# A fused graph and expert layer on one core: the head's clearing, statistics and copies in another order

## The chip, the cores and the metric

The kernel runs on one core of a Trainium2 chip. Its five engines are TensorE (PE), VectorE (DVE), ScalarE (ACT), GpSimd (POOL) and SyncE (SP); each works through its own instruction stream in order, and they wait for each other through semaphores. Transfers run on 16 DMA engines. SP and ACT put theirs on hardware queues (q1 and q10 in the profile), POOL puts its indirect ones (gathers and scatters by a list of row numbers) on q0. The metric is the device time of one execution in microseconds (us), lower is better. Times of the trace are counted from the start of the profiled span.

## What is computed

6250 nodes with 256 features each, 100,000 edges (src, dst) sorted by dst. First a graph layer, then a mixture of 8 experts of which each row uses the best 2:

```python
def gnn(h, edge_index, W, b):
    msg_sum = segment_sum(h[src], dst, num_segments=n)
    deg = segment_sum(ones, dst, num_segments=n)
    agg = msg_sum / maximum(deg, 1.0)[:, None]
    return concatenate([h, agg], axis=1) @ W.T + b

x = x + gnn(layernorm(x), stack([src, dst]), W, b)
x = x + ffn(layernorm(x)[None], gamma, beta, Wr, br, W1, b1, W2, b2)[0]
# ffn: logits = xn @ Wr + br; top 2; softmax of the two;
#      y = sum over chosen experts of w * (gelu(xn @ W1[e] + b1[e]) @ W2[e] + b2[e])
```

## The kernel before, in words

The nodes lie in 49 tiles of 128 rows (`NT` = 49; the last has 106). The program has a **head** (the five functions `sync_head`, `scalar_head`, `gpsimd_head`, `tensor_head`, `vector_head`) and a **stream** (`..._stream`), one loop over steps `t` that every engine runs in step with the others. There is no scheduler: the order on every engine is the order in which the code is written, and all waits are written out by hand.

In the stream's first 830 steps the sums over edges are made. Each step takes 128 edges: POOL gathers the 128 source rows of the normalised features out of the DRAM tensor `h_rows` (L631), PE multiplies them with a one-hot matrix of the edges' targets (L737), DVE adds the 128x257 result to the accumulator `acc` of the target tile (L1080; column 257 counts edges). The first 96 steps are of a special kind: two steps share one gather (48 gathers, into `shared`). From then on each step has its own gather, at most 17 ahead of the adds. DVE makes the one-hot matrices for 8 or 9 steps at a time (`one_hot`, L972). When a tile's sums are complete, the graph layer's product (L750), the second normalisation, the choice of experts, and later the experts themselves (L805, L830) follow for it between the steps. The rest of the stream hangs on the steps by fixed distances in `t`, so that nothing of it starts by the clock.

The head has three strands, which meet before the first gather of the stream:

- **The index strand.** POOL writes four index tables (`iotas`, L606 to L609) and clears all of `acc` (L610). DVE builds constants out of the tables (L866 to L875), then waits for `s_fst`, the first target of each block of 128 edges, which ACT's queue has loaded with L510 and L512 (672 and 109 elements of 4 bytes each). From L877 on, DVE and PE by turns work out where each tile's edges begin, until DVE writes `e_idx` (L933). In between DVE does the statistics of x tiles. POOL then gathers the edge tables, 8 gathers out of `comb` into `tab_i` (L616). They are converted to floats (targets by DVE, L954; sources by ACT, L537), transposed by PE (L706, L711) and written by DVE as `rel` (L960) and `srcs` (L964). The signal `srcs_up` says that `srcs` is there.
- **The normalisation strand.** SP loads x in 7 groups of 7 tiles (L439, L441). For each group `tile_stats` on DVE takes the statistics (7 + 7 instructions, L842 and L847), ACT takes the root (L526), `tile_scales` on DVE the reciprocal and the product (L854, L855; it stands after the second L842 of the next group), ACT writes 7 normalised tiles into one of two staging buffers `hst` (L532) and SP stores them to `h_rows` (L444). ACT waits at group b for the store of group b-2, whose buffer it fills again (L529).
- **The copies.** After the seven stores SP copies x to the DRAM tensor `x_rows` in seven parts (L447), which the graph layer reads later. POOL's stream waits for all seven stores, for `srcs_up` and for the second half of the transposed targets (L619 to L622). SP's stream waits for all copies before its first loads for the steps (L458).

## Time and profile before

| | us |
|---|---|
| runs, median of 3 | 1489.25 |
| runs, lowest and highest | 1487.42 and 1489.82 |
| the profiled execution, its own time | 1490.06 |
| its span (first to last instruction) | 1488.7 |
| PE busy | 1152.6 |
| POOL busy | 1082.9 |
| DVE busy | 770.8 |
| ACT busy | 496.9 |
| TensorE clock granted, mean | 0.907 |

The profiled execution took 1490.06 us, 1.36 us more than its span and 0.81 us more than the median of the runs. Busy time says how much an engine had to do; the head and the stream have different limits, so what the change is worth is read in the head, from which event released which. The rows of a timeline give start, duration, engine, line and operation, and in brackets how long the engine sat idle before and what released it. The name behind "q" (SPq, ACTq) is an engine's issue of a DMA; "us to landing" is from the issue to the arrival.

### The profile page before, as it was taken

Reading aid. Unit: us, or ns where it says so; the run is one execution under the profiler, and the core shown is the slowest. Engines: PE = TensorE matmul, PEld = TensorE weight load, DVE = VectorE, ACT = ScalarE, POOL = GpSimd, SP = SyncE. Lnnn points to the kernel's source line nnn. Section 1 sums busy time; section 2 is a strip of 40 time slices with the busy share of each in tenths; the row PEclk is TensorE's granted clock in tenths of the full one; section 3 lists DMA queues with packets and bytes.
Section 4 is the critical chain, followed back from the end, with each engine's and each line's share of the span. In section 5 each row is a group of like instructions: output and inputs, shape, how many; then the busy total and the mean of one; then the engine's idle time right before and its main releaser. Section 6 shows DMA issues by size and latency. Waiting matters only on the chain.

```text
span 1488.7 us, 22997 instructions
## 1 busy us (share of the span) xinstructions
PE 1152.6 (77%) x5570; PEld 876.0 (59%) x5570; DVE 770.8 (52%) x2634; ACT 496.9 (33%) x1095; POOL 1082.9 (73%) x1032
## 2 busy tenths in 40 slices
PE   3167888868876987688888768888897878877895
PEld 2033444536643776466667647666676766656794
DVE  8646654555564456435645544644646455554321
ACT  2400001303210453044336214414353434335573
POOL 3377477777777777777777777777777777773777
PEclk9999999789976999789999879979999998988998
DMA  8773475444434454444445454544555454453443
GB/s 257 223 258 106 141 221 182 127 125 136 119 115 130 134 136 114 121 132 119 134 122 136 113 128 127 133 116 124 135 122 128 121 130 123 121 125 92 71 68 40
DMA packets 125080, 197.46 MB, mean 133 GB/s; under 512 B 23954, under 2 KB 94023, under 8 KB 124711
## 3 DMA queue, kind: packets, MB, share of 16 engines
q0 software_dynamic: 63088, 130.30, 35.7%
q1 hardware_dynamic: 58325, 64.36, 13.8%
q10 hardware_dynamic: 3538, 1.34, 0.3%
q8 instruction: 50, 0.82, 0.2%
q14 instruction: 79, 0.65, 0.1%
HBM read 153.82 MB, written 49.27 MB: 136 GB/s over the span
## 4 chain that ended last, share of the span: by engine, by line
PE 44%; POOL 18%; issue 14%; DVE 11%; DMA 7%; ACT 3%; DVEq 1%; ACTq 0%; POOLq 0%; SPq 0%
PE psum L737 15%; PE psum L805 10%; PE psum L830 8%; POOL work L631 8%; DMA work<-h_rows,srcs 4%; PE psum L750 4%; DVE acc L1080 3%; POOL queue L640 3%; POOL region L631 2%; POOL out_dram L651 2%; POOL out_dram L659 2%; DMA out_dram<-expert_buf,tok_idx 1%; PE psum L751 1%; PE psum L784 1%; PE psum L817 1%
## 5 line engine op out<-in xcount | busy, mean ns | idle before, releaser
L631 POOL DMA_INDIRECT work<-h_rows,srcs x734 | 702.2, 957 | 236.9 <-issue 183.2
L1080 DVE TENSOR_TENSOR acc<-acc,psum 128x257 f32 x830 | 349.7, 421 | 521.1 <-PE psum L737 471.6
L737 PE MATMUL psum<-work 128*128 128x257 f32 x1468 | 477.5, 442 | 149.0 <-DMA work<-h_rows,srcs 76.3
L737 PEld LDWEIGHTS psum<-work 128*128 128x128 f32 x1468 | 274.4, 212 | 271.2 <-DMA work<-h_rows,srcs 127.7
L805 PEld LDWEIGHTS psum<-expert_buf 128*128 128x128 f32 x1680 | 226.7, 212 | 12.8 <-ACT expert_buf L589 5.2
L805 PE MATMUL psum<-expert_buf 128*128 128x128 f32 x1680 | 230.6, 296 | 3.0 <-ACT expert_buf L591 1.4
L830 PE MATMUL psum<-region,expert_buf 128*128 x840 | 201.7, 384 | 3.2 <-ACT expert_buf L591 3.2
L597 ACT ACTIVATE expert_buf<-psum,b_col 128x128 f32<-128x128 f32 x420 | 120.1, 370 | 208.2 <-PE psum L805 205.5
L830 PEld LDWEIGHTS psum<-region,expert_buf 128*128 128x128 f32 x840 | 154.6, 194 | 22.0 <-issue 4.6
L972 DVE TENSOR_TENSOR work<-psum,rel 128x1152 f32<-128x1152 f32 x98 | 126.3, 1289 | 52.5 <-PE psum L737 32.2
L651 POOL DMA_INDIRECT out_dram<-expert_buf,tok_idx x75 | 121.8, 1624 | 22.9 <-issue 21.6
L640 POOL DMA_INDIRECT queue<-pay,place_i x98 | 96.5, 984 | 48.6 <-issue 25.9
L544 ACT ACTIVATE acc<-acc,rdeg 128x256 f32<-128x256 f32 x49 | 25.1, 511 | 300.9 <-DVE rdeg L1086 300.9
L589 ACT COPY expert_buf<-region 128x1024 f32 x105 | 109.1, 1039 | 36.5 <-PE psum L805 31.3
L659 POOL DMA_INDIRECT out_dram<-expert_buf,tok_idx x60 | 93.6, 1560 | 35.9 <-issue 16.5
L601 ACT ACTIVATE expert_buf<-expert_buf,wcol 128x256 f32<-128x256 f32 x105 | 53.4, 509 | 169.6 <-DVE expert_buf L1147 168.4
L750 PE MATMUL psum<-wgt,pair_t 128*128 128x256 f32 x392 | 96.2, 390 | 1.2 <-ACT pair_t L548 1.2
L737 PE MATMUL psum<-region,work 128*128 x192 | 60.5, 440 | 44.1 <-issue 25.0
L750 PEld LDWEIGHTS psum<-wgt,pair_t 128*128 128x128 f32 x392 | 77.1, 197 | 14.0 <-ACT pair_t L548 2.4
L1147 DVE TENSOR_TENSOR expert_buf<-psum,b_bc 128x256 f32<-128x256 f32 x105 | 44.2, 421 | 78.9 <-PE psum L830 71.7
L737 PEld LDWEIGHTS psum<-region,work 128*128 128x128 f32 x192 | 32.0, 200 | 72.2 <-issue 70.6
L631 POOL DMA_INDIRECT region<-h_rows,srcs x48 | 45.8, 954 | 35.3 <-DMA h_rows<-region 20.9
(244 smaller groups left out, 924.4 us busy)
## 6 DMA issues: line engine op xcount, KB each, us to landing
expert_buf<-queue SPq DMA_DIRECT2D x105, 130.0 KB
work<-h_rows,srcs POOLq DMA_INDIRECT x734, 2.8
region<-in_L_ffn_W_dram SPq DMA_DIRECT2D x16, 512.0 KB, 6.3
h_rows<-region SPq DMA_DIRECT2D x7, 896.0 KB, 5.0
own<-h_rows SPq DMA_DIRECT2D x49, 128.0 KB
own<-x_rows SPq DMA_DIRECT2D x49, 128.0 KB
out_dram<-acc SPq DMA_DIRECT2D x49, 128.0 KB, 2.8
region<-in_x_dram SPq DMA_DIRECT2D x6, 896.0 KB, 11.5
```

The source lines that it names most:

```text
L589: w1c_up.up(act.copy(w1_now, w1_sb[:, ds(e, 1), :, :].rearrange("p a c h -> p (a c) h")))
L597: i = act.activation(gel[j % 2][:, k * P:(k + 1) * P], hidden(j)[:, k * P:(k + 1) * P], ACT.Gelu, bias=b1_col[:, ds(e + k * X, 1)])
L631: pool.indirect_dma_start(place_of(g)[:, 0:D], None, h_rows, bass.IndirectOffsetOnAxis(srcs[:, cell_of:cell_of + 1], 0)).then_inc(got[g % ...
L640: pool.indirect_dma_start(queue, bass.IndirectOffsetOnAxis(place_i[:, b % 2, n % 2, n // 2:n // 2 + 1], 0), pay[:, b % 2, n // 2, :], None ...
L651: pool.indirect_dma_start(out, bass.IndirectOffsetOnAxis(tok_idx[:, j % YB, 0:1], 0), ysb[j % YB], None, compute_op=ALU.add).then_inc(s_ad ...
L659: pool.indirect_dma_start(out_halves, bass.IndirectOffsetOnAxis(tok_idx[:, j % YB, side:side + 1], 0), ysb[j % YB][:, side * P:(side + 1) ...
L737: summed.up(pe.matmul(STEP_BANKS[t % BANKS][:, 0:GW], hot[:, k, :], rows, start=True, stop=True))
L750: pe.matmul(PAIR[:, 0:D], pair_t[:, c * P:(c + 1) * P], wgt[:, c, :], start=(c == 0), stop=False)
L805: i = pe.matmul(hidden(j)[:, units], w1_now[:, c, units], xt[j % 2][:, c * P:(c + 1) * P], start=(c == 0), stop=(c == DC - 1))
L830: i = pe.matmul(result(j), gel[j % 2][:, k * P:(k + 1) * P], w2_sb[:, ds(e, 1), k, :].rearrange("p a o -> p (a o)"), start=(k == 0), stop= ...
L972: hot_up.up(dve.tensor_tensor(hot[:, k0:k0 + n, :], COUNT[:, 0:P].unsqueeze(1).broadcast_to([P, n, P]), rel[:, first:first + n].unsqueeze( ...
L1080: added.up(dve.tensor_tensor(sums, sums, STEP_BANKS[t % BANKS][:, 0:GW], ALU.add))
```

## The change

- `acc` is cleared in two parts: POOL clears tiles 0 to 20 (5397 of 12593 elements per partition, signal `acc_clear`), ACT copies zeros from `zcol` into tiles 21 to 48 (7196 elements, signal `acc_zero`) after its last normalised group. DVE waits for both at the place where it waited for one.
- DVE does the statistics of groups 3 to 6, one after the other, and their scales before it reads the placed rows, copies `wgt` and converts the edge tables. The scales of group 1 are made at once after its statistics, where they stood inside those of group 2; those of group 2 stand inside group 3's.
- Both conversions of the edge tables are now DVE's, sources first; PE transposes sources first; ACT's eight copies are gone.
- PE's transposes of the graph layer's weights stand after the placing matmuls in place of before them.
- The load of those weights moves from ACT's queue to SP's, behind x. The five small loads (bias, gamma, beta, router) move from ACT's queue to SP's, behind the copies. PE's wait for them moves from the start of its stream to step 85, where they are used.
- SP's copies 0 to 3 stand behind stores 0 to 3, one behind each; copies 4 to 6 stay behind the last store.

```diff
+    CLEARED = 21
...
     def sync_head():
...
+        sp.dma_start(wg_sb, gnn_w.rearrange("(o p) i -> p o i", p=P)).then_inc(s_gw, 16)
         for b in range(NLB):
             h_up.wait(sp, b)
             sp.dma_start(h_rows[b * LB * P:(b + 1) * LB * P, :].rearrange("(t p) d -> p t d", p=P), hst[b % 2]).then_inc(s_hst[b % 2], 16)
-        for b in range(NLB):
-            rows = slice(b * LB * P, min((b + 1) * LB * P, N))
-            sp.dma_start(x_rows[rows, :], x[rows, :]).then_inc(s_xrows, 16)
+            if b < NLB - 3:
+                copy_x(b)
+        for b in range(NLB - 3, NLB):
+            copy_x(b)
+        sp.dma_start(gb_row, gnn_b.unsqueeze(0)).then_inc(s_small, 16)
...
     def scalar_head():
...
-        act.dma_start(wg_sb, gnn_w.rearrange("(o p) i -> p o i", p=P)).then_inc(s_gw, 16)
-        act.dma_start(gb_row, gnn_b.unsqueeze(0)).then_inc(s_small, 16)
...
             h_up.up(i)
-            if b == NLB - 3:
-                act.wait_ge(s_tab, 16 * GB)
-                for g in range(GB):
-                    src_f.up(act.copy(tab_f[0:GS, g, P:2 * P], tab_i[0:GS, g, P:2 * P]))
+        consts_up.wait(act)
+        acc_zero.up(act.copy(acc[:, CLEARED:NT, :], zcol[:, 0:1].unsqueeze(1).broadcast_to([P, NT - CLEARED, GW])))
...
-        acc_zero.up(pool.memset(acc[:, :, :], 0.0))
+        acc_clear.up(pool.memset(acc[:, 0:CLEARED, :], 0.0))
...
         srcs_up.wait(pool)
-        dst_t.wait(pool)
...
         tile_stats(1)
+        tile_scales(1)
         ranked.wait(dve)
...
-        tile_stats(2)
+        tile_stats(2, scales=False)
...
-        tile_stats(3)
+        for b in range(3, NLB):
+            tile_stats(b)
+        tile_scales(NLB - 1)
         placed.wait(dve, 1)
...
-        tile_stats(4)
         wgt_t.wait(dve)
...
-        tile_stats(5)
         dve.wait_ge(s_tab, 16 * GB)
         for g in range(GB):
+            src_f.up(dve.tensor_copy(tab_f[0:GS, g, P:2 * P], tab_i[0:GS, g, P:2 * P]))
+        for g in range(GB):
             dst_f.up(dve.tensor_scalar(tab_f[0:GS, g, 0:P], tab_i[0:GS, g, 0:P], w128[0:GS, g:g + 1], None, ALU.subtract))
-        tile_stats(6)
-        tile_scales(6)
...
         acc_zero.wait(dve)
+        acc_clear.wait(dve)
```

On SP the instructions between the load of x and the stream's first loads stood so before:

```order
L439 DMA region<-in_x_dram 128x6x256
L441 DMA region<-in_x_dram 106x256
L444 DMA h_rows<-region 128x7x256 x7
L447 DMA x_rows<-in_x_dram 16x14336 x6
L447 DMA x_rows<-in_x_dram 16x13984
L452 DMA expert_buf<-in_L_ffn_b_dram 8x512
```

and stand so now (a second and third pair of store and copy are left out):

```order
L441 DMA region<-in_x_dram 128x6x256
L443 DMA region<-in_x_dram 106x256
L444 DMA pay<-in_L_gnn_W_dram 128x2x512
L447 DMA h_rows<-region 128x7x256
L460 DMA x_rows<-in_x_dram 16x14336
...
L447 DMA h_rows<-region 128x7x256 x3
L460 DMA x_rows<-in_x_dram 16x14336 x2
L460 DMA x_rows<-in_x_dram 16x13984
L452 DMA singles<-in_L_gnn_b_dram 1x256
L453 DMA gam<-in_L_ffn_gamma_dram 128x2x1
```

Four copies have moved in front of later stores, three are left behind the last one, and the weights' load and the small loads have joined the same queue.

On DVE, at the end of the statistics of group 1 (L842 to L849) and the start of the ranking (L903), before:

```order
L842 BN_STATS stats<-region 128x6 x5
L847 BN_AGGR pay<-stats 128x2 x7
L849 TENSOR_SCALAR pay<-pay 128x7
L903 COPY pay<-psum 49x2
L904 COPY pay<-psum 49x1
```

and now:

```order
L846 BN_STATS stats<-region 128x6 x5
L851 BN_AGGR pay<-stats 128x2 x7
L853 TENSOR_SCALAR pay<-pay 128x7
L858 RECIPROCAL pay<-pay 128x7
L859 SCALAR_TENSOR_TENSOR pay<-pay 128x7
L908 COPY pay<-psum 49x2
```

The reciprocal of group 1, which needs ACT's root, now stands in front of the ranking.

On DVE from the conversion of the targets (L954) to the end of the head's table work, before:

```order
L954 TENSOR_SCALAR expert_buf<-expert_buf,pay 111x128 x8
L842 BN_STATS stats<-region 128x6 x2
L854 RECIPROCAL pay<-pay 128x7
L855 SCALAR_TENSOR_TENSOR pay<-pay 128x7
L842 BN_STATS stats<-region 128x6 x5
L847 BN_AGGR pay<-stats 128x2 x7
L849 TENSOR_SCALAR pay<-pay 128x7
...
L960 CAST rel<-psum 128x444 x2
L964 CAST srcs<-psum 128x444 x2
```

and now, from the scales of the last group on:

```order
L853 TENSOR_SCALAR pay<-pay 128x7
L858 RECIPROCAL pay<-pay 128x7
L859 SCALAR_TENSOR_TENSOR pay<-pay 128x7
L944 TENSOR_SCALAR singles<-psum 1x30x17
...
L955 COPY wgt<-psum 128x512 x2
L959 CAST expert_buf<-expert_buf 111x128 x8
L961 TENSOR_SCALAR expert_buf<-expert_buf,pay 111x128 x8
L964 CAST srcs<-psum 128x444 x2
L968 CAST rel<-psum 128x444 x2
```

The last group's statistics stood behind the conversion and have moved in front of it, and with them the work on the placed rows and on `wgt` has moved behind all statistics.

## Rows read from the trace of the kernel before

**Rows 1.** The page: shares of the chain of work that ended last, by engine.

```profile
PE 44%; POOL 18%; issue 14%; DVE 11%; DMA 7%; ACT 3%; DVEq 1%; ACTq 0%; POOLq 0%; SPq 0%
```

**Rows 2.** Windows: PE, PEld, DVE, ACT, POOL busy, granted clock, DMA share, GB/s.

```profile
68.45:171.00 102.55, 67.59 (x218) 36.22 (x219) 59.44 (x124) 0.00 (x0) 67.72 (x71) 0.98 0.55 181
171.00:400.00 229.00, 188.48 (x718) 122.16 (x717) 124.51 (x342) 48.02 (x97) 173.49 (x179) 0.88 0.52 152
400.00:800.00 400.00, 320.12 (x1573) 244.69 (x1572) 202.47 (x665) 129.59 (x287) 307.70 (x303) 0.90 0.48 127
```

**Rows 3.** Chain in order of time, end of the head: start, us, what.

```profile
63.17 5.02 DMA h_rows<-region
```

**Rows 4.** Timeline of POOL: clearing, first table gather, first gather of the stream.

```profile
1.93 10.58 POOL L610 MEMSET acc<- 128x12593 f32 x1
...
34.19 1.57 POOL L616 DMA_INDIRECT expert_buf<-comb,e_idx  x1 [21.68 <-DVE e_idx L933]
...
68.45 0.97 POOL L631 DMA_INDIRECT region<-h_rows,srcs  x1 [20.95 <-DMA h_rows<-region]
```

**Rows 5.** Timeline of DVE in the head.

```profile
2.02 10.58 DVE L866 CAST iota<-work 128x128 f32<-128x128 int32 x1
...
13.27 0.16 DVE L877 CAST work<-work 112x7 f32<-112x7 int32 x1
...
24.84 0.15 DVE L903 COPY pay<-psum 49x2 f32<-49x2 f32 x1
...
52.83 1.66 DVE L954 TENSOR_SCALAR expert_buf<-expert_buf,pay 111x128 f32<-111x128 int32 x8 [3.80 <-DMA expert_buf<-comb,e_idx]
```

**Rows 6.** Timeline of ACT: roots (L526) and normalised groups (L532).

```profile
25.97 0.19 ACT L526 ACTIVATE pay<-pay 128x7 f32<-128x7 f32 x1
...
55.48 3.55 ACT L532 ACTIVATE region<-region,pay 128x256 f32<-128x256 f32 x7 [0.85 <-DVE pay L855]
...
59.60 3.55 ACT L532 ACTIVATE region<-region,pay 128x256 f32<-128x256 f32 x7 [0.47 <-DVE pay L855]
```

**Rows 7.** DMA packets of ACT's queue from 8.50 to 8.75 us: count, MB, share.

```profile
q10 hardware_dynamic: 3, 0.00, 1.0%
```

**Rows 8.** The lines of stores (L444) and copies (L447): issues and landings.

```profile
L444 SPq DMA_DIRECT2D h_rows<-region x7: 372/372/389, 26.1 to 63.2; - x7
...
DMA to landing us min/median/max: 4.0/5.0/7.0
...
L447 SPq DMA_DIRECT2D x_rows<-in_x_dram x7: 589/589/1365, 63.6 to 68.4; - x7
...
DMA to landing us min/median/max: 7.3/13.3/19.9
```

**Rows 9.** Windows around the first store, all columns as in rows 2.

```profile
25.00:27.00 2.00, 0.00 (x0) 0.00 (x0) 1.86 (x19) 1.16 (x4) 0.00 (x0) 1.00 0.15 49
27.00:30.00 3.00, 0.88 (x5) 0.88 (x6) 2.93 (x11) 0.00 (x0) 0.00 (x0) 1.00 0.94 314
```

**Rows 10.** DVE windows 38.5:41, 44.3:45.6, 52.8:54.4, 59.4:61.7, 63.2:65.4: their sum.

```profile
sum 9.90, DVE 9.44; mean DVE 1.89
```

**Rows 11.** DMA issues of the stream's gathers at 69 to 70 and at 120 to 121 us: landing.

```profile
region<-h_rows,srcs POOLq DMA_INDIRECT x2, 13.5
...
region<-h_rows,srcs POOLq DMA_INDIRECT x1, 2.7
```

**Rows 12.** Timeline of DVE: adds of steps 0, 8, 17 and 25.

```profile
82.82 0.42 DVE L1080 TENSOR_TENSOR acc<-acc,psum 128x257 f32 x1 [13.35 <-PE psum L737]
...
92.64 0.42 DVE L1080 TENSOR_TENSOR acc<-acc,psum 128x257 f32 x1 [0.21 <-DVE acc L1080]
...
101.25 0.41 DVE L1080 TENSOR_TENSOR acc<-acc,psum 128x257 f32 x1
...
106.30 0.42 DVE L1080 TENSOR_TENSOR acc<-acc,psum 128x257 f32 x1 [0.21 <-DVE acc L1080]
```

**Rows 13.** The page: ACT's copies of 1024 elements, group by line.

```profile
L589 ACT COPY expert_buf<-region 128x1024 f32 x105 | 109.1, 1039 | 36.5 <-PE psum L805 31.3
```

More of the change, by code:

```diff
@@ L701, in tensor_head @@
         placed.up(pe.matmul(psum[7][:, 0:NT], coef[0:NT, 1:2].broadcast_to([NT, P]), order[0:NT, 0:NT], start=True, stop=True))
+        pe.wait_ge(s_gw, 16)
+        for c in range(2 * DC):
+            for o_ in range(2):
+                i = pe.transpose(psum[4 + c // 2][:, (c % 2) * D + o_ * P:(c % 2) * D + (o_ + 1) * P],
+                                 wg_sb[:, o_, c * P:(c + 1) * P], ident[:, :])
+        wgt_t.up(i)
         wgt_up.wait(pe)
         rows_up.wait(pe)
+        for g in range(GB):
+            src_f.wait(pe, g)
+            i = pe.transpose(psum[6 + g // 4][:, (g % 4) * GS:(g % 4 + 1) * GS], tab_f[0:GS, g, P:2 * P], ident[0:GS, 0:GS])
+            if g in (3, GB - 1):
+                src_t.up(i)
         for g in range(GB):
@@ L708, in tensor_head @@
                 dst_t.up(i)
-        for g in range(GB):
-            src_f.wait(pe, g)
-            i = pe.transpose(psum[6 + g // 4][:, (g % 4) * GS:(g % 4 + 1) * GS], tab_f[0:GS, g, P:2 * P], ident[0:GS, 0:GS])
-            if g in (3, GB - 1):
-                src_t.up(i)
     def tensor_stream():
@@ L752, in tensor_stream @@
             if t == 85:
+                pe.wait_ge(s_small, 16 * 5)
                 beta_up.wait(pe)
@@ L842, in tile_stats @@
             i = dve.bn_stats(stats[:, j, :], xall[:, b * LB + j, :])
-            if j == 1 and b:
+            if j == 1 and b and scales:
                 tile_scales(b - 1)
@@ L950, in vector_head @@
         wgt_up.up(i)
-        tile_stats(5)
         dve.wait_ge(s_tab, 16 * GB)
         for g in range(GB):
+            src_f.up(dve.tensor_copy(tab_f[0:GS, g, P:2 * P], tab_i[0:GS, g, P:2 * P]))
+        for g in range(GB):
             dst_f.up(dve.tensor_scalar(tab_f[0:GS, g, 0:P], tab_i[0:GS, g, 0:P], w128[0:GS, g:g + 1], None, ALU.subtract))
-        tile_stats(6)
-        tile_scales(6)
-        placed.wait(dve, 1)
+        for part, (lo, hi) in enumerate(((0, 4), (4, GB))):
+            src_t.wait(dve, part)
+            i = dve.tensor_copy(srcs[:, lo * GS:hi * GS], psum[6 + part][:, 0:(hi - lo) * GS])
+        srcs_up.up(i)
         for part, (lo, hi) in enumerate(((0, 4), (4, GB))):
@@ L961, in vector_head @@
         d_own.up(i)
-        for part, (lo, hi) in enumerate(((0, 4), (4, GB))):
-            src_t.wait(dve, part)
-            i = dve.tensor_copy(srcs[:, lo * GS:hi * GS], psum[6 + part][:, 0:(hi - lo) * GS])
-        srcs_up.up(i)
         h_up.wait(dve, NLB - 1)
```

23 lines of the change are left out of this document (10 added, 13 removed).

## The prediction

> **What bounds the kernel now.** I read the chain of waits first. Over the whole span PE holds 44% of it and POOL 18% [rows 1], but the change touches the head alone, so I looked in the windows for where the head ends and what follows it. From 171 us on PE is busy for about four fifths of the time [rows 2], and nothing there is started by the clock: every wait is tied to a step. The stream should therefore be moved as a block by as much as its first steps move. What counts is when the first gather of the stream goes out, and when the adds run at their own pace.
>
> The chain at the head's end says that the first gather (68.45) is released by the last store of normalised rows, which took 5.0 us [rows 3, 4]. Behind it comes a second loss that the chain does not show as such: the first gather is issued at 68.45 and the first add runs at 82.82 [rows 4, 12], since gathers issued then land after 13.5 us, while one at 120 us lands after 2.7 [rows 11]. In that time the seven copies of x run: the first is issued at 63.6 and the last, issued at 68.4, lands 19.9 us later at 88.3 [rows 8]. Only then do the adds find their data. From step 8 (92.64) on they run at the pace that DVE sets. Steps 17 to 25 took 106.30 - 101.25 = 5.05 us [rows 12], so with that pace from the start step 0 would have stood at 92.64 - 5.05 = 87.6. This is the **effective start** of the sums, and the whole question is where it goes.
>
> **The index strand.** DVE's cast at 2.02 ends together with POOL's clearing of `acc`, after 10.58 us [rows 4, 5]. With 5397 of 12593 elements POOL is done in 10.58 x 5397 / 12593 = 4.5 us, so 6.05 us sooner. By that L877 would move from 13.27 to 7.2. But L877 needs the block targets, 781 elements of 4 bytes on ACT's queue. Three packets of that queue still ran between 8.50 and 8.75 us [rows 7], and the next quarter has none of it. I take 9.2 for their landing, an estimate, so L877 gains 4.1 us, not 6.05 (bounds: 6.05 if the small packets come sooner, 2 if the semaphore comes 2 us after the last packet).
>
> The Trainium skill ("SBUF — State Buffer", section "SBUF: two separate sides") says that DVE and GpSimd share a port pair as an exclusive lock, and that the loser is blocked for the whole instruction. By that rule alone the strand would gain the full 6.05 us; rows 7 say that 4.1 of it can be used, and the sum goes by the rows.
>
> The scales of group 1 now stand in front of the ranking. They need ACT's root, which ACT began at 25.97 behind seven normalised tiles, while DVE went on at 24.84 [rows 5, 6]. So DVE waits 26.16 - 24.84 = 1.3 us and spends 0.45 on the two operations before the ranking: 1.75 us. The table gathers start at 34.19 - 4.1 + 1.75 = 31.8. Before, DVE had all tables at 52.83, 18.6 us after the first table gather [rows 4, 5]; now at about 50.5, and DVE asks for them later still (below), so the tables don't bind.
>
> **The normalisation strand.** After `e_idx`, at 31.5, DVE does four groups in a row. A scale needs the root, the root stands behind ACT's seven tiles, and these need the scale before: one group takes 59.60 - 55.48 = 4.12 us [rows 6]. The scale of group 2 comes 1.15 us after `e_idx`, at 32.7. Unhindered, the scale of group 6 comes at 32.7 + 4 x 4.12 = 49.2, its rows are ready at 52.8, and with 5.0 us for the store [rows 8] the stream could start at 57.8.
>
> It is hindered by the queue. SP's queue now holds stores and copies in turn, and ACT may not refill a buffer before the store of two groups ago has landed. One store takes 0.94 x 3 = 2.8 us of all DMA engines [rows 9]. One copy takes (88.3 - 70.9) / 6 = 2.9 us from landing to landing (70.9 is 63.6 + the shortest 7.3) and (88.3 - 64) / 7 = 3.5 us if all is charged to it [rows 8]; I take 3.1. After the load of x, at 25.5, the queue runs: store 0 to 28.3, copy 0 to 31.4, store 1 to 34.2, copy 1 to 37.3, store 2 to 40.1, copy 2 to 43.2, store 3 to 46, copy 3 to 49.1, store 4 to 51.9. The table gathers carry 0.9 MB in the same time, about one more store's worth, and I put 2 us of it before store 3 and 0.7 behind. Store 3 has then landed at 48.3 and store 4 at 55. Group 5 starts on ACT at 48.3 in place of 45.1, and the scale of group 6 comes at 52.4. Group 6 starts at 55, is ready at 58.5, and its store lands 5 us later, at 63.5. Some of the queue's work fits into gaps that I have charged in full (25 to 27 us had a DMA share of 0.15 [rows 9], where store 0 can begin), so I take **62.5** for the first gather, 6 us earlier than before. The bounds are 57.8 (no hindrance) and 65 (3.5 us per copy).
>
> DVE's other table work hides under this. From the scale of group 6 at 52.4 it is 9.9 us, by the sum of five stretches (placed rows, `wgt`, targets, `rel` and `srcs`, constants) [rows 10], and 1.6 for the source conversions, which cost like the targets [rows 5]. So `srcs` is there at about 60.5, and the one-hot matrices for step 0 at 66 to 69. The clearing by ACT takes 7196 elements: 1039 ns for 1024 [rows 13] against 507 for 256 (3.55 / 7 [rows 6]) is 0.69 ns per element, so 5.3 us, from 58.5 to 63.8, where DVE arrives at about the same time. These are free while the first gather's data land after 69; if the data came at 65 they would be next.
>
> **The copies that are left.** Three copies stand behind the last store. They run from 62 to 62 + 3 x 3.1 = 71.3. Gathers issued into seven copies landed after 13.5 us, by when four or five copies had gone [rows 8, 11]; with three left the first gather lands when they end. From landing to the first add I allow 1.4 us (before, 82.82 less 68.45 + 13.5 is 0.9 [rows 11, 12], and the copies end at slightly different times on the 16 engines), and for a start from rest 0.6 us, both estimates. The effective start is then 73.3, against 87.6: **14.3 us less**, of which 6 come from the earlier store and 8.3 from four copies out of the gathers' way. The small loads and `b2` follow the copies on SP's queue; by then several gathers are out and a step needs half of one, so I put them at nothing. Before, SP's next loads fell behind the last copy at 88.3 too, and from step 8 on the adds kept their pace [rows 12].
>
> A sentence of the Trainium skill speaks against the change ("DMA: Bandwidth & Descriptors", section "Queues, rings and completion order"): an engine takes the descriptors of one ring in order, so a copy in front of a store delays it in full. If the queue never ran empty, the seven stores, four copies and the tables would end at 25.5 + 7 x 2.8 + 4 x 3.1 + 2.7 = 60.2, which is inside the bounds above; the sum already pays for this rule. No stretch of the trace of before has copies in front of stores.
>
> **Sum.** 1490.06 - 14.3 = 1475.8, made against the profiled execution. That one lies 0.8 above the median of the runs, so 1475.0 to 1475.8 is meant, and I say 1475.5.
>
> **Rivals.** (1) The three copies left starve the first gathers as seven did: 13.5 us to landing and no full pace before. Then the first add is at 62.5 + 14.4 = 76.9, the effective start at 77.5, and the time 1480. For it: the same mix of queues as in rows 11. Against: there is less in the queue. 15%. (2) The queue has no such price: ACT is never held up, the first gather goes out at 57.8, the copies end at 67, the effective start is 69, and the time 1471.5. For it: the unused DMA time in rows 9. 13%. (3) ACT and the queue hold each other up more than I think, so that each store waits for a copy and each group for a store, and the first gather goes out at 66 to 68. The effective start is then 77 to 79 and the time about 1481. 7%. (4) The gain is lost later. PE's granted clock was 0.88 from 171 to 400 us and 0.90 from 400 to 800 [rows 2]. PE holds 44% of 1488.7 us of the chain [rows 1], 655 us; a mean clock lower by 0.01 of 0.907 costs 7 us. From 0.02 on it eats the 14.3 us, and at 0.03 the time is 1497, **slower** than before. For it: the clock isn't constant. Against: the change alters nothing of PE's work after the head. 5% for slower, 4% for within 0.2%. (5) The order of the copies changes nothing for the gathers, since something else holds them (a slow start of POOL's queue). Then only 6 us remain: 1484. Against: 2.7 us in rows 11. 3%.
>
> **How the numbers follow.** The forecast has 53%, its own range is 1472.5 to 1478.5. Faster by over 0.2% (3 us, about what a measurement of this kernel can tell from no change): the forecast, rivals 1, 2, 3 and 5, 91%. Same 4%, slower 5%. For 8 in 10 the range takes in rivals 1 and 2 and most of 3: 1468 to 1482.
>
> **What would show it.** Right: the cast that was L877 at 9 to 9.5 us; the first table gather at 31 to 32.5; groups 3 to 6 on ACT 4.1 us apart until one waits for a store, at group 5 or 6; the last store landing at 61 to 64; copies ending at 70 to 72; the first add at 71 to 74 and no pause after it. From 171 us on the stages should have their old busy times, shifted. Wrong: a last store after 66, gathers that land after 13 us again, or a clock in the stages of rows 2 that is off by more than 0.01.

## The result, and the profile after

| | before | after |
|---|---|---|
| median of the runs | 1488.65 us (4 runs, 1487.42 to 1489.82) | 1478.14 us (4 runs, 1474.95 to 1478.98) |
| ratio, 95% interval | | 0.9923 [0.9911, 0.9935] |
| profiled execution | 1490.06 us, span 1488.7 | 1477.89 us, span 1476.6 |
| mean granted clock | 0.907 | 0.904 |

The changed kernel is 10.5 us faster by the medians and 12.2 us by the profiled executions. The forecast was 1475.5 us, that is 13.2 and 14.3 us; the measured median lies inside the range that went with it (1472.5 to 1478.5), 0.4 us below its upper end.

The timeline of POOL after (start, us, engine, line, operation, idle time before and what ended it) answers to [rows 4]:

```profile
1.93 4.59 POOL L615 MEMSET acc<- 128x5397 f32 x1
...
30.36 1.57 POOL L621 DMA_INDIRECT expert_buf<-comb,e_idx  x1 [23.84 <-DVE e_idx L938]
...
63.52 0.97 POOL L635 DMA_INDIRECT region<-h_rows,srcs  x1 [19.85 <-DMA h_rows<-region]
```

The clearing is 6.0 us shorter, the first table gather 3.8 us earlier, the first gather of the stream 4.9 us earlier. The timeline of DVE after answers to [rows 5, 12]; its lines are the old ones plus 4 or 5:

```profile
2.01 4.58 DVE L870 CAST iota<-work 128x128 f32<-128x128 int32 x1
...
7.77 0.17 DVE L881 CAST work<-work 112x7 f32<-112x7 int32 x1 [0.41 <-DMA work<-in_dst_dram]
...
20.70 0.20 DVE L858 RECIPROCAL pay<-pay 128x7 f32<-128x7 f32 x1 [1.25 <-ACT pay L533]
...
64.58 0.29 DVE L1071 COPY psum<-iota 128x128 f32<-128x128 f32 x1 [1.63 <-ACT acc L542]
...
74.67 0.42 DVE L1085 TENSOR_TENSOR acc<-acc,psum 128x257 f32 x1 [6.88 <-PE psum L740]
...
80.40 0.42 DVE L1085 TENSOR_TENSOR acc<-acc,psum 128x257 f32 x1 [0.21 <-DVE acc L1085]
```

These are the start constants, the cast of the block targets, the scales of group 1, DVE's wait for ACT's clearing, and the adds of steps 0 and 8. The first add comes 8.15 us earlier (74.67 for 82.82), the add of step 8 12.24 us earlier (80.40 for 92.64), so the effective start is 75.35 for 87.6. The timeline of ACT answers to [rows 6]. It shows the load of ACT's function table, the normalised groups 2 to 6 with what ended ACT's idle time before each, and ACT's clearing:

```profile
13.11 1.28 ACT L533 ACT_TABLE_LOAD   x1 [13.11 <-issue]
...
31.59 3.55 ACT L539 ACTIVATE region<-region,pay 128x256 f32<-128x256 f32 x7 [3.00 <-DMA h_rows<-region]
...
37.54 3.55 ACT L539 ACTIVATE region<-region,pay 128x256 f32<-128x256 f32 x7 [2.30 <-DMA h_rows<-region]
...
42.51 3.55 ACT L539 ACTIVATE region<-region,pay 128x256 f32<-128x256 f32 x7 [1.32 <-DMA h_rows<-region]
...
49.10 3.55 ACT L539 ACTIVATE region<-region,pay 128x256 f32<-128x256 f32 x7 [2.95 <-DMA h_rows<-region]
...
54.87 3.55 ACT L539 ACTIVATE region<-region,pay 128x256 f32<-128x256 f32 x7 [2.12 <-DMA h_rows<-region]
58.32 6.18 ACT L542 COPY acc<-zcol 128x7196 f32<-128x7196 f32 x1
```

Every group from 2 to 6 now waits for a store, where groups 5 and 6 waited for a scale of DVE's before [rows 6]. The stores (L447) and copies (L460), with the time from issue to landing, answer to [rows 8]:

```profile
L447 SPq DMA_DIRECT2D h_rows<-region x7: 372/378/696, 22.1 to 58.4; - x7
...
DMA to landing us min/median/max: 4.1/7.9/12.1
...
L460 SPq DMA_DIRECT2D x_rows<-in_x_dram x7: 571/828/2643, 22.8 to 60.9; - x7
...
DMA to landing us min/median/max: 7.2/10.3/13.6
```

A store behind a copy takes 7.9 us instead of 5.0; the copies are quicker, 10.3 for 13.3. The chain by engine and the windows (columns as in rows 2) answer to [rows 1, 2]:

```profile
PE 48%; POOL 15%; issue 13%; DVE 10%; DMA 7%; ACT 4%; DVEq 1%; SPq 1%; ACTq 0%; POOLq 0%
```

```profile
171.00:400.00 229.00, 184.30 (x713) 119.14 (x712) 123.82 (x343) 48.44 (x99) 174.44 (x180) 0.88 0.52 152
400.00:800.00 400.00, 325.01 (x1597) 251.62 (x1597) 202.03 (x668) 135.59 (x297) 307.71 (x303) 0.90 0.48 127
```

The clock is 0.88 and 0.90 in both stages, as before. From the effective start to the span's end it is 1488.7 - 87.6 = 1401.1 us before and 1476.6 - 75.35 = 1401.3 after: the stream was moved as a block, and the difference is the head's. That the two agree to 0.2 us is in part luck: in the experiments on chips with the usual clock this stretch took 1398.9 (e11) to 1403.3 us (e1).

### The profile page after: what moved, and what is told of

The parts are those of the page before. It is cut to its first block, busy times and chain, and to the rows that moved or that the text cites. A ratio compares the mean times of both kernels' runs of the same rounds, so it can differ in the third digit from the quotient of the medians.

```text
span 1476.6 us, 22997 instructions
## 1 busy us (share of the span) xinstructions
PE 1149.7 (78%) x5570; PEld 875.2 (59%) x5570; DVE 765.4 (52%) x2642; ACT 501.1 (34%) x1088; POOL 1076.1 (73%) x1032
## 4 chain that ended last, share of the span: by engine, by line
PE 48%; POOL 15%; issue 13%; DVE 10%; DMA 7%; ACT 4%; DVEq 1%; SPq 1%; ACTq 0%; POOLq 0%
PE psum L740 15%; PE psum L809 12%; PE psum L834 10%; POOL work L635 7%; DMA work<-h_rows,srcs 5%; PE psum L753 4%; POOL region L635 3%; DVE acc L1085 3%; POOL queue L644 3%; DMA h_rows<-region 2%; POOL out_dram L655 2%; PE psum L754 2%; PE psum L788 1%; PE psum L821 1%; POOL out_dram L663 1%
## 5 line engine op out<-in xcount | busy, mean ns | idle before, releaser
L809 PEld LDWEIGHTS psum<-expert_buf 128*128 128x128 f32 x1680 | 225.2, 211 | 12.8 <-ACT expert_buf L594 4.9
L834 PE MATMUL psum<-region,expert_buf 128*128 x840 | 206.0, 390 | 3.0 <-ACT expert_buf L596 3.0
L1152 DVE TENSOR_TENSOR expert_buf<-psum,b_bc 128x256 f32<-128x256 f32 x105 | 44.2, 421 | 79.1 <-PE psum L834 71.3
L821 PE MATMUL psum<-ident,expert_buf 128*128 128x128 f32 x210 | 43.8, 292 | 34.6 <-DVE expert_buf L1152 31.3
```

The costliest lines, as they stand in the source:

```text
L809: i = pe.matmul(hidden(j)[:, units], w1_now[:, c, units], xt[j % 2][:, c * P:(c + 1) * P], start=(c == 0), stop=(c == DC - 1))
L834: i = pe.matmul(result(j), gel[j % 2][:, k * P:(k + 1) * P], w2_sb[:, ds(e, 1), k, :].rearrange("p a o -> p (a o)"), start=(k == 0), stop= ...
```

## The experiments

All kernels compute everything. "Start" is the effective start, the add of step 8 less 5.05 us. The events are read from one profiled execution each, the median is that of 4 or 5 runs.

| kernel | first table gather | first gather | first add | start | median us | ratio [95%] |
|---|---|---|---|---|---|---|
| before | 34.19 | 68.45 | 82.82 | 87.6 | 1488.65 | |
| after | 30.36 | 63.52 | 74.67 | 75.35 | 1478.14 | 0.9923 [0.9911, 0.9935] |
| e1 copies behind | 30.59 | 59.88 | 73.82 | 80.9 | 1482.85 | 0.9955 [0.9941, 0.9969] |
| e2 six in front | 30.81 | 64.36 | 71.78 | 72.2 | 1475.24 | 0.9903 [0.9882, 0.9925] |
| e3 POOL clears all | 35.84 | 68.09 | 79.20 | 80.2 | 1482.90 | 0.9950 [0.9934, 0.9967] |
| e4 copies late | 31.25 | 59.49 | 65.56 | 66.4 | 1467.91 | 0.9856 [0.9838, 0.9874] |
| e9 split and copies on before | 30.90 | 67.84 | 78.88 | 79.6 | 1479.01 | 0.9933 [0.9915, 0.9951] |
| e10 loads on ACT | 31.84 | 64.79 | 76.68 | 77.1 | 1478.60 | 0.9924 [0.9905, 0.9944] |
| e11 fill the waits | 30.61 | 60.47 | 66.48 | 67.35 | 1467.62 | 0.9851 [0.9835, 0.9868] |
| e12 third buffer | 30.41 | 57.65 | 63.65 | 64.1 | 1465.31 | 0.9849 [0.9824, 0.9875] |

The experiments used three chips. On the first (e1 to e4, e9, e12) the kernel before took 1489.62 us beside e1 to e4 and 1489.38 beside e9 and e12; on another (e10, e11) it took 1489.95. A third one, for e5 to e8, was much slower; see below.

### e1: all copies behind the stores

The changed kernel with its copies where they were.

```
             sp.dma_start(h_rows[...], hst[b % 2]).then_inc(s_hst[b % 2], 16)
-            if b < NLB - 3:
-                copy_x(b)
-        for b in range(NLB - 3, NLB):
+        for b in range(NLB):
             copy_x(b)
```

> The changed kernel with all seven copies of x behind the last store again. Theory (the adds begin when SP's queue has run empty; a copy in front of a store delays the store, but one behind delays the first gathers): ACT is no longer held up by stores, groups 3 to 6 come 4.1 us apart, the first gather goes out at 56 to 58 in place of 63.5, but seven copies end at 80 to 82, so the effective start of the adds is 79 to 81 in place of 75.4, and the time about 1482.5. Rival A (what counts is when the first gather goes out): 7 us earlier, 1471. Rival B (the copies' place is of no weight, the index strand's gain is all): 1478.

The first gather went out at 59.88, later than expected, since ACT still waited for stores twice: 2.98 us before group 2 (at 31.80) and 2.83 us before group 4 (at 42.40, while the table gathers ran). The time agrees with the forecast. DVE's timeline shows the first add, those of steps 3 and 4, and behind it stand the first gather and those issued at 63 to 64 us (count, median us to landing):

```profile
73.82 0.42 DVE L1083 TENSOR_TENSOR acc<-acc,psum 128x257 f32 x1 [9.87 <-PE psum L738]
...
76.38 0.42 DVE L1083 TENSOR_TENSOR acc<-acc,psum 128x257 f32 x1 [0.43 <-PE psum L738]
82.56 0.42 DVE L1083 TENSOR_TENSOR acc<-acc,psum 128x257 f32 x1 [5.75 <-PE psum L738]
```

```profile
region<-h_rows,srcs POOLq DMA_INDIRECT x1, 10.7
...
region<-h_rows,srcs POOLq DMA_INDIRECT x2, 17.8
```

The gather issued at 63.70 lands at 81.5, and the sums stand still for 5.75 us. So the four copies in front of stores cost the first gather 63.52 - 59.88 = 3.6 us and bring the effective start 5.6 us forward. The copies, not a slow start of POOL's queue (rival 5), hold the gathers.

### e2: six copies in front

```
-            if b < NLB - 3:
+            if b < NLB - 1:
                 copy_x(b)
-        for b in range(NLB - 3, NLB):
+        for b in range(NLB - 1, NLB):
             copy_x(b)
```

> The changed kernel with six copies between the stores (behind stores 0 to 5) and one behind the last. Theory (the queue's total counts): the first gather goes out at 69 to 71, the one copy left ends at 73 to 75, the effective start is 74.5 to 76.5, the time 1477 to 1479.5, the same within the noise. Rival A (the first gather counts): 6.5 us later, 1484.5. Rival C (each copy left behind the last store costs 2 us or more, those in front cost nothing): 1474 or less.

The theory that only the queue's total counts failed. Two more copies in front cost the first gather 64.36 - 63.52 = 0.8 us, while the effective start fell by 3.1 us. The first rows are POOL's first gather and DVE's first add in e2. Behind them stands what gathers took to land, first the one issued at 64.36 alone, then the mean of those whose issue ran between 65 and 66 us:

```profile
64.36 0.97 POOL L635 DMA_INDIRECT region<-h_rows,srcs  x1 [20.23 <-DMA h_rows<-region]
...
71.78 0.42 DVE L1085 TENSOR_TENSOR acc<-acc,psum 128x257 f32 x1 [3.85 <-PE psum L740]
```

```profile
region<-h_rows,srcs POOLq DMA_INDIRECT x1, 4.2
...
region<-h_rows,srcs POOLq DMA_INDIRECT x2, 3.6
```

In the changed kernel the gathers issued at 64 to 65 us took 7.0. From the first gather to the effective start it is 21.0 us with seven copies behind the last store (e1), 11.8 with three, 7.9 with one and 6.9 with none (e4, below): a copy left behind costs 2.3 us between seven and three, 2.0 between three and one, and 1.0 as the last one. A copy moved in front costs the first gather 0.4 us here and 0.9 in e1. The queue has gaps there: in the changed kernel the store behind each of the four copies was issued 2.5, 9.1, 5.5 and 4.6 us after that copy, when ACT had its rows ready.

### e3: POOL clears all of acc

```
-    CLEARED = 21
+    CLEARED = NT
...
-        consts_up.wait(act)
-        acc_zero.up(act.copy(acc[:, CLEARED:NT, :], zcol[...].broadcast_to([...])))
...
-        acc_zero.wait(dve)
         acc_clear.wait(dve)
```

> The changed kernel with all of the accumulator cleared by POOL at the start, as before, and no clearing by ACT. Theory: the index strand loses 5.5 us (the cast of the block targets at 13.3 in place of 7.8, the first table gather at 35 to 36), but the queue of stores and copies hides most of it: first gather at 64 to 66, effective start 76 to 77.5, time 1479 to 1480.5. Rival B (the earlier index strand is the gain): the effective start moves by the full 5.5 us, 1483.5. Rival D (ACT's clearing at the end of the head holds DVE and costs 1.6 us): without it the time falls, 1476.5.

The block targets' cast stands at 13.27 again, 5.5 us later than in the changed kernel. The expectation that the queue hides most of it failed, and its rival B (1483.5) was near: the first gather is 4.6 us later, the effective start 4.9, the median 4.8. The stores do land sooner, which wins back little:

```profile
L447 SPq DMA_DIRECT2D h_rows<-region x7: 372/378/395, 26.1 to 63.0; - x7
...
DMA to landing us min/median/max: 4.5/5.7/9.1
```

The whole strand, the first store included (issued at 26.1 for 22.1), is shifted; the queue is no fixed stop that the stores run up against.

### e4: copies inside the stream

The copies go out after the sums of step 10, 20 and so on to 70, the wait for them and the first loads of x1's rows at step 85.

```
-            if b < NLB - 3:
-                copy_x(b)
-        for b in range(NLB - 3, NLB):
-            copy_x(b)
...
             if t == -1:
-                sp.wait_ge(s_xrows, 16 * NLB)
...
-            for r in [0] if t == -1 else [...]:
+            if 0 < t <= 10 * NLB and t % 10 == 0:
+                summed.wait(sp, t)
+                copy_x(t // 10 - 1)
+            if t == 85:
+                sp.wait_ge(s_xrows, 16 * NLB)
+            for r in [0] if t == 85 else [...]:
```

> The changed kernel with no copy of x in the head: SP issues copy b when step 10(b+1) of the stream has been multiplied, and loads the first tile's own rows at step 85. Theory: as in the kernel with all copies behind, the first gather goes out at 56 to 58, and its data land after 3 to 4 us; the first add is held next by DVE's one-hot matrices at 60 to 61, the effective start is 61.5 to 63, 13 us earlier than in the changed kernel. If the copies in the stream stall no gather that is due, 1465; if each stalls the adds by a part of its 3 us, up to 1470. Rival E (the copies' DMA time is paid wherever they stand, since the adds wait for gathers that queue behind them): 1478.

It is 10.2 us faster than the changed kernel, by the start 9.0. The time is in the expected range, the head is not: the first gather came at 59.49 and the start at 66.4, 3.4 us later than expected. Though no copy is in the head, ACT waited for stores before groups 4 and 5 (1.16 and 2.57 us), which e12 takes up. In the stream a copy lands after 5.5 us (issued between 72 and 125 us: six and one, us to landing at the end), and the adds keep pace beside it:

```profile
x_rows<-in_x_dram SPq DMA_DIRECT2D x6, 896.0 KB, 5.5
...
x_rows<-in_x_dram SPq DMA_DIRECT2D x1, 874.0 KB, 5.3
```

With no copy about, gathers land after 2.8 us, and the chain of waits (start, us, what) runs over another piece, ACT's clearing:

```profile
55.11 6.09 ACT acc L542
...
61.28 0.30 DVE psum L1071
...
61.61 1.37 DVE work L976
...
64.19 5.96 PE psum L740 x16
```

### e5 to e8: the parts one by one, on a chip with a lower clock

These four ran on another chip, on which the kernel before took 1800.47 us. Their times can't be compared with the others (see the last section). Their heads can be read to about 1 us: e7 and e9 are one kernel on two chips, with the first gather at 67.12 and 67.84 and the add of step 8 at 84.80 and 84.61. That the last two agree so well is luck, since from step 0 to step 8 it took 6.9 us here and 5.7 there. e5 splits the clearing in the kernel before, and nothing else:

```
+    CLEARED = 21
...
+        consts_up.wait(act)
+        acc_zero.up(act.copy(acc[:, CLEARED:NT, :], zcol[...].broadcast_to([...])))
...
-        acc_zero.up(pool.memset(acc[:, :, :], 0.0))
+        acc_clear.up(pool.memset(acc[:, 0:CLEARED, :], 0.0))
...
         acc_zero.wait(dve)
+        acc_clear.wait(dve)
```

> The kernel before with one part of the change alone: POOL clears tiles 0 to 20, ACT clears the rest after its last group. Theory (what the index strand gains goes through to the end in full, as losing it did in the kernel where POOL clears all): the cast of the block targets at 7.8 to 8.7 in place of 13.3, tables, first gather and effective start 4.6 to 5.5 us earlier (first gather 63 to 64, effective start 82 to 83 against 87.6), time 1483.5 to 1484.5. Rival (the head before is bound by stores and copies, the index strand is slack): within 1.5 us of the kernel before, 1488.

The first gather went out at 64.72 (3.7 us earlier), the add of step 8 at 88.83 (3.8 earlier, with a granted clock of 0.73 from 85 to 90 us, so the effective start may be earlier than this shows). The cast, the first gather and the effective start (83.8) all came 0.7 to 0.8 us behind their expected ranges. The cast of the block targets was at 9.53, against 7.77 in the changed kernel and 7.51 to 8.67 in the others: the landing of that small load varies by 2 us. The ratio was 1.0007 [0.9984, 1.0031].

e6 moves the copies in the kernel before, and nothing else:

```
             sp.dma_start(h_rows[...], hst[b % 2]).then_inc(s_hst[b % 2], 16)
-        for b in range(NLB):
-            rows = slice(b * LB * P, min((b + 1) * LB * P, N))
-            sp.dma_start(x_rows[rows, :], x[rows, :]).then_inc(s_xrows, 16)
+            if b < NLB - 3:
+                copy_x(b)
+        for b in range(NLB - 3, NLB):
+            copy_x(b)
```

> The kernel before with another part alone: copies 0 to 3 stand behind stores 0 to 3, the other three behind the last store. Theory: the copies fill gaps between the stores and delay the tables by 0.5 to 3 us (first gather at 69 to 71.5 against 68.5), but with three copies left the effective start follows the first gather by 11.8 us in place of 19.1, so it is 81 to 83.3 against 87.6, time 1482.5 to 1485. Rival (DMA time is conserved, the tables' delay eats the gain): 1488 or more.

The first gather went out at 71.16, 2.7 us later, and the add of step 8 at 88.82, 3.8 us earlier; ratio 1.0033 [0.9996, 1.0070]. The effective start of 83.8 is 0.5 us behind the expected range, the time doesn't show the gain on this chip. So the copies alone have both signs in one trace, and the net in the head is a gain.

e7 has both edits, on the kernel before, and e9 is the same kernel on the first chip.

> The kernel before with both parts, that is the changed kernel without the new order of DVE's statistics and conversions and without the moved loads. Theory (the two parts add up): the effective start 9.5 to 11.5 us earlier than before, at 76 to 78, time 1477.5 to 1480; then the new order on DVE is worth 0 to 2 us of the 12.2. Rival (the new order is needed, since the tables' conversion holds the last group's statistics): effective start 80 or later, 1482 or more.

> The same kernel as the one with clearing split and copies between, but not the new order on DVE nor the moved loads. It stood on a chip whose TensorE was held down to a granted clock of 0.50 for some 70 us after step 8, which left only the head to be read: first gather at 67.1. Expected from that head, with 11.8 us from first gather to effective start as in the changed kernel: effective start 78.5 to 79.5, time 1481 to 1482.5. Rival (the two parts are all of the change): 1478.

e7: first gather 67.12, add of step 8 84.80, ratio 0.9979 [0.9951, 1.0008]. e9: 67.84 and 84.61, 8.0 us less than before at step 8; the two parts give 3.8 + 3.8 apart. What the changed kernel has beyond e9 is worth 4.3 us at the first gather and 4.2 at step 8: DVE's new order, the conversion of the sources on DVE, PE's order, POOL's dropped wait for the targets, and the moved loads. The times don't show it, though: 1479.01 for 1478.14, intervals of about 2.7 and 1.8 us to either side. The expectation of 1481 to 1482.5 for e9 missed, and its time is nearer to the rival's 1478 (the two parts are all of the change); only the head speaks against that rival. e9's stream took 1399.1 us from its effective start, 2.2 less than the changed kernel's.

### e10: the six loads back on ACT's queue

The change moved six loads of weights from ACT's queue to SP's. This undoes it in the changed kernel.

```
-        sp.dma_start(wg_sb, ...).then_inc(s_gw, 16)
...
-        sp.dma_start(gb_row, gnn_b.unsqueeze(0)).then_inc(s_small, 16)
...
         act.dma_start(comb[FULL_ROWS:ET, P:P + REST], ...).then_inc(s_pads, 16)
+        act.dma_start(wg_sb, ...).then_inc(s_gw, 16)
+        act.dma_start(gb_row, gnn_b.unsqueeze(0)).then_inc(s_small, 16)
...
```

> The changed kernel with the six loads (layer weights and the five small ones) back in ACT's queue at their old place. Theory: ACT cannot load its table before their issue is done (16.6 to 17.9 us in place of 13.1 to 14.4), so the first root comes about 2 us later, the table gathers and everything behind them 1.7 to 2 us later: first table gather at 32 to 32.5 against 30.4, first gather at 65 to 65.7 against 63.5, time 1479.5 to 1480.5. Rival (the place of the loads is of no weight, as the prediction had it): first gather at 63.5, 1478.

ACT's function table is loaded at 16.53, and group 0 starts at 18.50 instead of 17.02:

```profile
16.53 1.28 ACT L533 ACT_TABLE_LOAD   x1 [16.53 <-issue]
...
18.50 3.55 ACT L539 ACTIVATE region<-region,pay 128x256 f32<-128x256 f32 x7 [0.47 <-DVE pay L859]
```

The first gather is at 64.79, 1.3 us later than in the changed kernel, the effective start 1.8 us. The first table gather (31.84) and the first gather stand 0.2 us before the expected ranges. The time, 1478.60, doesn't resolve it. This leaves 4.2 - 1.8 = 2.4 us of the head to DVE's order and the rest, by subtraction; no run has them alone.

### e8 and e11: work in ACT's waits

One kernel, run as e8 on the slow chip and as e11 on one with the usual clock: e4, with ACT's clearing after group 1, where ACT waits for DVE, and the placed rows and `wgt` ahead of DVE's last scale.

```
             h_up.up(i)
-        consts_up.wait(act)
-        acc_zero.up(act.copy(acc[:, CLEARED:NT, :], zcol[...].broadcast_to([...])))
+            if b == 1:
+                consts_up.wait(act)
+                acc_zero.up(act.copy(acc[:, CLEARED:NT, :], zcol[...].broadcast_to([...])))
...
-        tile_scales(NLB - 1)
         placed.wait(dve, 1)
...
         wgt_up.up(i)
+        tile_scales(NLB - 1)
```

> The kernel with the copies in the stream, and two pieces of work moved into waits: ACT clears its part of the accumulator between groups 1 and 2, where it waits 6 us, and DVE reads the placed rows and copies the weights in front of the last group's scales, where it waits 3.4 us. Theory: the sources are there 3.3 us earlier, DVE is done with its constants at 58, and the first add is held by the first gather's data alone: first gather at 59 to 60, first add at 63.5 to 64.8 in place of 65.6, time 1466 to 1467.5. Rival (the waits were no slack, the moved work pushes ACT's groups back): first gather later than 60.5, 1469 or more.

> The same kernel as the one that fills the waits, which stood on the chip with the held-down clock. From its head there (first gather at 60.2, first add at 66.2, no better than 59.5 and 65.6 without the filling) the first add waits for the first gather's data, not for DVE: effective start 66 to 67, time 1467 to 1469, the same as with copies in the stream alone. Rival (the first add waited for DVE's one-hot matrices, and gains their 3 us): effective start below 65, 1466 or less.

e8: first gather 60.18, first add 66.16, where 63.5 to 64.8 was expected; ratio 0.9983 [0.9955, 1.0011] with the clock held down. e11: 60.47 and 66.48, later than e4's 59.49 and 65.56 by 1 us, and 1467.62 us for 1467.91: no difference, as expected for e11. The clearing fits into the wait (24.84 to 31.0, group 2 at 31.59), so that piece of e4's chain is gone, but the data of the first gather are now next, at the same time, and group 6 waits 2.31 us for the scale that stands later.

### e12: a third buffer for the stores

e11 with a third staging buffer, in `b2_bc`, which is loaded only later.

```
-    hst = [None, None]
+    hst = [None, None, b2_bc[:, :, :].rearrange("p a b -> p (a b)")[:, 0:LB * D].rearrange(...)]
+    HB = 3
...
-            if b >= 2:
-                act.wait_ge(s_hst[b % 2], 16 * (b // 2))
+            if b >= HB:
+                act.wait_ge(s_hst[b % HB], 16 * (b // HB))
```

> The kernel with copies in the stream and filled waits, and a third staging buffer for the normalised groups (in the space of the experts' bias table, which is loaded later), so that ACT waits for the store of three groups ago. Theory: what delays the last store in the changed kernel is ACT's wait for one of two buffers, not the DMA engines' total work; without it groups 3 to 6 come 4.1 us apart, the last group begins at 48 to 49 in place of 51.6 to 52.2, the first gather goes out at 56 to 57.5 in place of 59.5 to 60.2, and the effective start is at 62.5 to 64 in place of 66.4; time 1464 to 1466 on a chip on which the kernel before takes 1489. Rival (the DMA engines are full between 32 and 55 us, the stores only queue longer): first gather at 59 or later.

ACT's groups 3, 4 and 6 and POOL's first gather in e12:

```profile
35.51 3.55 ACT L540 ACTIVATE region<-region,pay 128x256 f32<-128x256 f32 x7 [0.47 <-DVE pay L861]
39.63 3.55 ACT L540 ACTIVATE region<-region,pay 128x256 f32<-128x256 f32 x7 [0.47 <-DVE pay L861]
...
49.70 3.55 ACT L540 ACTIVATE region<-region,pay 128x256 f32<-128x256 f32 x7 [2.31 <-DVE pay L861]
```

```profile
57.65 0.97 POOL L637 DMA_INDIRECT region<-h_rows,srcs  x1 [13.93 <-DMA h_rows<-region]
```

No group waits for a store, and groups 2 to 5 stand 4.12 us apart, the pace of the loop through DVE and ACT. The effective start is 64.1, 3.2 us before e11's, and the time 1465.31 us is the best of all: 24 us below the kernel before, 12.8 below the changed one. Against e11, which ran on another chip (1467.62, intervals of 3.8 and 2.5 us), the gain in time is inside what the intervals allow for none; the head shows it.

## Why the prediction was right, and where it was off

**The frame held.** The effective start moved by 12.24 us, the profiled execution by 12.2. The experiments, median and effective start against the changed kernel: e1 +4.7 and +5.6, e2 -2.9 and -3.1, e3 +4.8 and +4.9, e4 -10.2 and -9.0, e9 +0.9 and +4.2, e10 +0.5 and +1.8, e11 -10.5 and -8.0, e12 -12.8 and -11.2. A median is uncertain by 2 to 4 us here, so all but e9 agree within that, and e9 is at its edge. The slower side (rival 4) didn't come: the clock in both stages was the old one.

**The signs.** Of the signs that were named, the last store landed at 63.26 (61 to 64), the copies ended at 71.3 (70 to 72), no pause followed the first add, and the clock stayed. The cast (7.77 for 9 to 9.5), the first table gather (30.36 for 31 to 32.5), the groups on ACT and the first add (74.67 for 71 to 74) came otherwise.

**The index strand.** The cast was at 7.77, predicted 9.2; e5 shows that 9.5 occurs as well. DVE's first cast ended with the clearing, at 6.59. The Trainium skill ("SBUF — State Buffer", section "SBUF: two separate sides") has DVE blocked for the whole of GpSimd's instruction where both need the port pair that they share, and these rows agree: 4.58 us beside a clearing of 4.59. The wait for ACT's root before the ranking was 1.25 us (predicted 1.3). The first table gather came at 30.36 instead of 31.8, and this gain was used, as e3 shows.

**The normalisation strand.** The mechanism was right: ACT is held up by stores that haven't landed. Group 5 started at 49.10 (predicted 48.3), group 6 at 54.87 (55), the first gather went out at 63.52 (62.5). But ACT waited for a store at every group from 2 on, not only at 5 and 6, for 1.3 to 3.0 us each. "Groups 4.1 us apart until one waits for a store" was wrong; this is what rival 3 described, without its late first gather. That the sum came out near is luck in part: the strand had started sooner, which made up for the waits. Two things start it sooner, the cast at 7.77 and a term that was **missing**: ACT's queue without six loads, 3.4 us at the function table, 1.3 at the first gather and 1.8 at the start (e10). The prediction put the moved loads at nothing. It looked at the queue to which they go, and not at the one that they leave. Its sum of the queue also gives 48.0 and 54.6 for the landings of stores 3 and 4 as it is written, where it goes on with 48.3 and 55.

**The rule on ring order.** The Trainium skill ("DMA: Bandwidth & Descriptors", section "Queues, rings and completion order") says that an engine consumes the descriptors of one ring in ring order. From this the prediction drew that a copy in front of a store delays it in full. The stores do take 7.9 us for 5.0. But four copies of 2.9 us or more delayed the last store by 3.6 us in all (e1 against the changed kernel). The prediction took it for a queue that is never empty, and this one had gaps between a copy and the next store (see e2).

**From the copies to the first add.** This is the mis-sized term. The three copies were to end at 71.3, and so they did: the last was issued at 60.9 and took 10.4 us. Two deviations cancel in this, a first gather 1.0 us late and copies that ended 7.8 us behind it and not 8.8. The second gather, issued at 64.80, landed 7.0 us later at 71.8, so it was also right that the first gathers land when the copies end. But the first add was put 1.4 us behind the copies' end (72.7) and came 3.4 us behind it (74.67). These 2.0 us are the whole 2.05 us by which the effective start was late (75.35 for 73.3).

SP's first load for the steps, at 74.81, is no sign of a late copy. The profile gives as the end of SP's wait a store of zeros that stands behind the copies on the same queue. The rows are the last copy's landing, SP's wait (total, times, longest) and PE's first matmul, all in the changed kernel:

```profile
x_rows<-in_x_dram SPq DMA_DIRECT2D x1, 874.0 KB, 10.4
...
SPq L474 <- DMA x_rows<-xn_t: 8.4, 1, 8.4
...
73.30 8.36 PE L740 MATMUL psum<-region,work 128*128 x24 [13.45 <-issue]
```

In three kernels the trace has the landing of the first gather itself, and the time from there to the first add is the same, with long gathers and short ones:

| kernel | first gather issued | lands after | lands at | PE's first matmul | first add | landing to add |
|---|---|---|---|---|---|---|
| e1 | 59.88 | 10.7 | 70.6 | 72.44 | 73.82 | 3.2 |
| e2 | 64.36 | 4.2 | 68.6 | 70.41 | 71.78 | 3.2 |
| e12 | 57.65 | 2.8 | 60.4 | 62.27 | 63.65 | 3.2 |

It is 1.8 us from the landing to PE's first matmul and 1.4 from there to the add. The prediction had 1.4 for both, out of 0.9 read from [rows 11, 12], and that reading was wrong. The 13.5 us belong to the second gather, issued at 69.73, which landed at 83.2, after the first add at 82.82. They were counted from 68.45, the issue of the first. With 3.2 in place of 1.4 the prediction's own sum gives an effective start of 75.1 and a time of 1477.6.

**The clearing by ACT** took 6.18 us, predicted 5.3, and DVE waited 1.63 us for it at 64.58. The 0.69 ns per element came from two unlike operations, a copy of 1024 elements and an activation on 256; this copy took 6.18 us / 7196 = 0.86. It stayed hidden, as was said. e4 shows the price once that cover is gone: it is then on the chain.

**The split of the gain.** The prediction gave 6 us to the earlier store and 8.3 to the copies. Taken one after the other (before, e1, changed kernel), all the rest gives 6.7 and the copies 5.6. Taken the other way (e6, e9, changed kernel) it is 3.8 for the copies, 4.2 for the split clearing and 4.2 for order and loads together, with 1 us of doubt on e6.

**What stays open.** What fills the 1.8 us between a landing and PE's first matmul isn't shown: the profile names no releaser ("issue"), and the one-hot matrices were ready before the landing in all three kernels of the table. At that place the program has PE read the row numbers of 17 steps into registers, which no run took apart. Why a gather waits so long is only suggested. Before, the DMA engines began 32 packets with 0.92 MB between 69 and 70 us, 16 of them under 512 B, so the other 16 have some 57 KB each. How these and the gathers' small ones take turns on an engine was not measured apart. That the gain of 4.2 us over e9 in the head doesn't show in the times was not followed up.

## What to carry to other kernels

When a bulk transfer stands behind the last store that gates a stream, price it twice: by what it costs the store if it goes in front, where the queue has gaps, and by what it costs the first small transfers if it stays behind, here 0.4 to 0.9 us against 1.0 to 2.3. Then ask whether it belongs there at all: put into the stream, the copies cost nothing that could be measured, and that was worth almost as much as the whole change. When the time from a landing to the first use is read off a trace, make sure that both rows belong to the same transfer. And when instructions are moved from one queue to another, read what stands behind them on the queue that they leave.

## What the hardware showed that was not expected

**A chip on which TensorE's clock is held down.** The kernel before took 1800.47 us there and 1489 to 1490 us on the other two. Windows of e5 on it (columns as in rows 2), and behind them those of the kernel before on the first chip:

```profile
68.00:100.00 32.00, 11.93 (x30) 7.42 (x30) 7.06 (x14) 0.00 (x0) 24.08 (x27) 0.86 0.90 304
100.00:110.00 10.00, 2.44 (x4) 1.00 (x4) 0.85 (x2) 0.00 (x0) 7.57 (x8) 0.50 0.37 105
...
160.00:170.00 10.00, 7.54 (x27) 3.87 (x26) 6.69 (x17) 0.00 (x0) 0.00 (x0) 1.00 0.00 1
```

```profile
100.00:110.00 10.00, 7.73 (x27) 3.79 (x26) 7.57 (x15) 0.00 (x0) 7.58 (x8) 1.00 0.36 105
```

From 100 to 110 us the granted clock was 0.50, the lower level (1.2 GHz), and PE ran 4 matmuls in 10 us where it runs 27 at 1.00 (2.4 GHz). POOL issued 8 gathers in both, and the DMA engines moved 1.05 MB in both, so PE wasn't short of data. Seven times fewer matmuls at half the clock means that something besides the clock held PE back; the profile doesn't say what. In e8 the first add stands 16.7 us earlier than in the kernel before on a chip with the usual clock, which would be a ratio of 0.991 there, and 0.9983 [0.9955, 1.0011] was measured: at least half of the head's gain is lost again. For e7, with 8 us (a ratio of 0.9956), 0.9979 [0.9951, 1.0008] decides nothing. A small gain in a head has to be measured where PE runs freely.

**A long copy between DRAM and DRAM starves a gather on another queue.** Gathers took 2.8 us with none about (e4), 7.0 behind three (the changed kernel), and behind seven 13.5 (before, the second gather) to 17.8 (e1, the fourth).
